# Attention on one Trainium2 core: products with V in one burst, and the transpose of y in y's own bank

## The reference, cut to what matters

```python
q = (xn @ q_w + q_b).reshape(Bx, Tx, H, -1)
k = (xn @ k_w + k_b).reshape(Bx, Tx, H, -1)
att = jnp.einsum('bnhl,bmhl->bnmh', q, k)
att = att + (1.0 - mask) * -1000000.0
att = jax.nn.softmax(att, axis=2)
v = ((xn @ v_w + v_b) * src_mask[:, :, None]).reshape(Bx, Tx, H, -1)
y = jnp.einsum('bnmh,bmhl->bnhl', att, v).reshape(Bx, Tx, Dx)
```

## Time and profile before

| | us |
|---|---|
| median of 3 runs | 7056.02 |
| lowest and highest of them | 7052.95, 7059.61 |
| the profiled execution, its own time | 7056.06 |
| its span in the profile | 7054.2 |

### The profile page before, as it was taken

One profiled execution on the slowest core, in us unless ns is written; L12 is line 12 of the kernel. 1 busy time (PEld: TensorE's weight loads), 2 busy tenths in 40 slices (PEclk: granted clock), 3 DMA queues, 4 the chain that ended last, 5 costly groups with the idle time before them and its releaser, 6 DMA issues.

```text
span 7054.2 us, 136215 instructions
## 1 busy us (share of the span) xinstructions
PE 6300.6 (89%) x43360; PEld 3962.4 (56%) x43360; DVE 5911.7 (84%) x7137; ACT 4676.3 (66%) x6657; POOL 3153.6 (45%) x1541
## 2 busy tenths in 40 slices
PE   6998899988999889989799898998899988999888
PEld 2664457644575546745467455764457544575544
DVE  0787988789897998979888799888988799897985
ACT  2665668567685677847777467765768667685674
POOL 0105871067601775019730388105771067601873
PEclk9999899998999989999899999999899998999989
DMA  3525884368923687237862388525884368923786
GB/s 143 165 81 160 192 209 125 108 162 187 235 76 137 160 200 209 73 134 177 202 181 91 131 197 204 148 87 158 187 209 126 116 159 188 239 68 132 169 195 166
DMA packets 437182, 1108.91 MB, mean 157 GB/s; under 512 B 50185, under 2 KB 50313, under 8 KB 432225
## 3 DMA queue, kind: packets, MB, share of 16 engines
q1 hardware_dynamic: 256672, 671.49, 29.1%
q0 software_dynamic: 161344, 394.81, 28.4%
q10 hardware_dynamic: 18432, 33.56, 1.3%
HBM read 581.17 MB, written 250.10 MB: 118 GB/s over the span
## 4 chain that ended last, share of the span: by engine, by line
PE 62%; issue 14%; DVE 7%; DMA 6%; POOL 5%; ACT 4%; DVEq 0%; SPq 0%; ACTq 0%; POOLq 0%
PE ps L1245 38%; PE ps L1490 10%; PE ps L1354 7%; POOL area_s L699 5%; DMA area_acc<-area_w 4%; PE ps L1295 4%; ACT area_h L839 2%; DMA z_keep<-z_st 2%; DVE area_s L1065 2%; DVE area_h L1182 1%; PE ps L1297 1%; ACT area_s L830 1%; DVE area_dt L1170 1%; PE ps L1439 1%; DVE area_u L1173 1%
## 5 line engine op out<-in xcount | busy, mean ns | idle before, releaser
L699 POOL TENSOR_TENSOR area_s<-area_u,area_s 128x1024 f32<-128x1024 f32 x1024 | 2539.9, 2568 | 553.2 <-DVE area_u L1173 386.6
L1182 DVE TENSOR_TENSOR_SCAN area_h<-ps,area_s 128x1024 f32<-128x1024 f32 x1024 | 2335.2, 2280 | 58.3 <-POOL area_s L699 44.9
L1490 PEld LDWEIGHTS ps<-ident,area_h 128*128 128x128 f32 x8192 | 954.4, 146 | 917.7 <-DVE area_acc L1192 524.9
L830 ACT ACTIVATE area_s<-area_s,negmax 128x1024 f32<-128x1024 f32 x1024 | 1177.7, 1150 | 421.9 <-DVE negmax L1065 421.1
L1490 PE MATMUL ps<-ident,area_h 128*128 128x128 f32 x8192 | 1153.7, 286 | 300.6 <-DVE area_h L1182 205.7
L1065 DVE CUSTOM_DVE_ANT_0 area_s<-ps,area_dt 128x1024 f32<-128x1024 f32 x1024 | 1243.3, 1215 | 113.9 <-PE ps L1245 113.9
L686 POOL TENSOR_TENSOR area_s<-area_s 128x1024 f32<-128x1024 f32 x64 | 176.2, 2753 | 2504.5 <-ACT area_s L874 2504.5
L901 ACT ACTIVATE ps<-area_dt,negA 128x1024 f32<-128x1024 f32 x1024 | 1146.3, 1120 | 221.9 <-DVE area_h L1182 108.0
L887 ACT ACTIVATE area_w<-ps,C_nat 128x512 f32<-128x512 f32 x1024 | 704.4, 688 | 733.2 <-PE ps L1490 685.6
L1354 PE MATMUL ps<-ident,area_s 128*128 128x128 f32 x8192 | 1129.0, 276 | 17.3
L1354 PEld LDWEIGHTS ps<-ident,area_s 128*128 128x128 f32 x8192 | 939.6, 142 | 246.7 <-ACT area_h L839 74.2
(11 more groups left out here) (126 smaller groups left out, 5555.5 us busy)
## 6 DMA issues: line engine op xcount, KB each, us to landing
area_acc<-area_w POOLq DMA_DIRECT2D x256, 1024.0 KB, 8.9
area_s<-b_rows SPq DMA_DIRECT2D x256, 512.0 KB, 5.2
q_stack<-qk_keep SPq DMA_DIRECT2D x520, 128.0 KB, 2.8
k_stack<-qk_keep SPq DMA_DIRECT2D x520, 128.0 KB, 3.1
qk_keep<-q_stack SPq DMA_DIRECT2D x144, 256.0 KB, 4.9
qk_keep<-k_stack SPq DMA_DIRECT2D x144, 256.0 KB, 4.9
area_s<-z_keep SPq DMA_DIRECT2D x72, 512.0 KB, 4.5
y_keep<-area_acc POOLq DMA_DIRECT2D x8, 4096.0 KB, 15.1
```

Source lines behind the costliest of these rows:

```text
L699: pool.tensor_tensor(dbu[:, dl % 2, :], U[:, k // (NS * DL) * DL + dl, :], bb[:, q, :], ALU.mult).then_inc(s_dbu.sem, 1)
L830: nc.scalar.activation(S[:, t % SR, :], S[:, t % SR, :], ACT.Exp, scale=-1.0, bias=negmax[:, t % TILES:t % TILES + 1], accum_out=den[:, t ...
L1182: v.tensor_tensor_scan(out=hs[:, q, dl, :], data0=banks(2 * (dl % 2)), data1=dbu[:, dl % 2, :], initial=0.0, op0=ALU.mult, op1=ALU.add).th ...
L1490: last = nc.tensor.transpose(ps[:, 4 + n % 2, dl * P:(dl + 1) * P], hs[:, r % 2, dl, n * P:(n + 1) * P], ident[:, :])
```

## The change

All eight key tiles of a half's product with V are now issued at step 0 as one burst (64 records), and nothing at steps 1 and 2. The transpose of y no longer takes a bank of the ring: it goes to columns 128 to 255 of bank 6, next to the product with V, and the normalising product reads it there. The ring then has only the two uses for every tile. Since the next half's product writes bank 6 too, its burst waits at step 0 for the normalising product of the half before (`s_yn`).

```diff
--- before.py
+++ after.py
@@ -43,9 +43,7 @@
     order = []
     for t in range(ALL):
         order += [("dve", t), ("act", t)]
-        if t >= 2 * HALF - 1 and t % HALF == HALF - 1:
-            order.append(("y", t // HALF - 1))
-    return order + [("y", ALL // HALF - 1)]
+    return order
 
 
 RING_ORDER = ring_order()
@@ -55,7 +53,7 @@
 def ring_bank(*use):
 
     return RING[RING_AT[use] % len(RING)]
-AV_KEYS = ((0, 1, 2), (3, 4, 5), (6, 7), ())
+AV_KEYS = ((0, 1, 2, 3, 4, 5, 6, 7), (), (), ())
 
 
 N0_STEP, QKV_STEP, QKV_SPAN = 5, 9, 51
@@ -1073,7 +1071,7 @@
                         dve.wait_ge(*s_rd.at(b, half + 1))
                         at = t % TILES
                         v.tensor_tensor(Y[:, hf * HALF:(hf + 1) * HALF, head * HD:(head + 1) * HD],
-                                        ps[:, ring_bank("y", half), 0:P].rearrange("p (c l) -> p c l", l=HD),
+                                        ps[:, 6, P:2 * P].rearrange("p (c l) -> p c l", l=HD),
                                         rden[:, at - 3:at + 1].unsqueeze(2).to_broadcast([P, HALF, HD]), ALU.mult
                                         ).then_inc(s_yn.sem, 1)
                     t = s - C_LAG
@@ -1335,7 +1333,7 @@
                 def ring_free(*use):
                     if RING_AT[use] >= len(RING):
                         who, i = RING_ORDER[RING_AT[use] - len(RING)]
-                        pe.wait_ge(*{"dve": s_pv, "act": s_pa, "y": s_yn}[who].at(b, i + 1))
+                        pe.wait_ge(*{"dve": s_pv, "act": s_pa}[who].at(b, i + 1))
 
                 scores(0)
                 scores(1)
@@ -1362,6 +1360,8 @@
                         if step == 0:
                             pe.wait_ge(*s_pv.at(b, (half + 1) * HALF))
                             pe.wait_ge(*s_pa.at(b, (half + 1) * HALF))
+                            if half:
+                                pe.wait_ge(*s_yn.at(b, half))
                         for m in AV_KEYS[step]:
                             for c in range(HG):
                                 last = mm(ps[c * HD:(c + 1) * HD, 6, 0:P], V[:, m, head * HD:(head + 1) * HD],
@@ -1372,8 +1372,7 @@
                     if t >= 0 and t % HALF == HALF - 1:
                         half = t // HALF
                         pe.wait_ge(*s_yc.at(b, half + 1))
-                        ring_free("y", half)
-                        nc.tensor.transpose(ps[:, ring_bank("y", half), 0:P], yT[:, half % 2, :], ident[:, :]
+                        nc.tensor.transpose(ps[:, 6, P:2 * P], yT[:, half % 2, :], ident[:, :]
                                             ).then_inc(s_yt.sem, 1)
                 pe.wait_ge(*s_yn.at(b, G * HG * 2))
                 norm_pe(n1, b)
```

## The result

The changed kernel takes 7158.21 us (median of 4 runs, 7157.27 to 7160.92) against 7055.46 of the kernel before (7052.95 to 7059.61): a ratio of 1.0147, 95% interval 1.0132 to 1.0162, so 102.75 us or 1.5% slower. The forecast was 7177, slower, with a range of 7070 to 7240.

The account below looks back on a forecast made before the run. PE was taken to bound the attention, DVE close behind. A loop through both engines grew the period from 8.55 to 9.06 us; 29 periods plus 0.3 a batch, times 8, gave 121 us more: 7177, range 7070 to 7240.

Parts of the forecast that it names:

- The saving on PE: Products with V on PE: two of three groups go, 0.30 us each, 0.60 off PE per period.
- Step 1 of the loop: Start of DVE's step 0 reduction, through the normalising product, to the start of PE's burst: 1.49 us.
- Step 2: On PE, from the start of the 64-record burst to the next scores: 1.89 us, bounds 1.79 and 2.16.
- Step 3: From those scores through four transposes to DVE's copy: 1.21 us, with DVE idle for 1.5.
- Step 4: DVE from that copy to the next period: 0.61 to the reduction, then DVE steps of 1.75 and 2.11 us.
- The sum: The whole loop through PE and DVE: a period of 9.06 us against 8.55 before, 0.51 more.
- Head and tail: Each attention batch outside its 29 periods, before and after them: 0.3 us more together.
- The other stages: Kernel stages outside the attention: not edited, no cost, no overlap with the attention's end.
- The added wait: At step 0 PE's burst waits about 0.5 us for DVE's normalising product of the half before.
- the case without any such wait: Rival: the normalising product is done before PE arrives, loop over DVE's copy of y, period 8.60, time 7070; chance 0.08.
- PE stays the bound: Rival: PE's own 7.65 us sets the attention period, 209 us less, 6847; chance 0.07.
- The clock: Rival: the clock falls to 1.2 GHz in stretches, doubling the burst's 1.89 us, over 7400; chance 0.03.

Follow-up runs that it names:

- e4: The change with key tiles back in groups of 3, 3 and 2 and the normalising product ahead of the reduction: 6971.63 us, period 8.21.
- e5: The change with two groups of four key tiles at steps 0 and 2 and the normalising product ahead of the reduction: 6900.78 us, 6899.06 when repeated.
- e8: The kernel before with only the key tiles regrouped, four each at steps 0 and 2, transposed y still in the ring: 6967.90 us, period 8.19.
- e3: The whole change with the normalising product moved ahead of the reduction in the same DVE step: 7047.13 us, period 8.55.
- e2: The change without the burst, groups of 3, 3 and 2 as before, transposed y in bank 6: 7068.42 us, period 8.61.
- e7: The whole change with one extra DVE copy of transposed y right ahead of the normalising product: 7208.87 us, period 9.22.
- e1: The kernel before with only the burst of eight key tiles at step 0, transposed y still in the ring: 7174.38 us, period 9.06.
- e6: The change with two groups of four key tiles at steps 0 and 1 and the normalising product ahead of the reduction: 7031.26 us, period 8.48.

## Why the prediction was right

- **What bounds it.** PE was full, DVE close behind. e4 shows it: with the ring's wait of 0.30 off PE's path, and no other wait put in its place, the same groups of 3, 3 and 2 take 8.21 instead of 8.55.
- **The saving on PE.** A group has a fixed cost and the records have a rate: put at 0.30 and 0.0275 us. e5 has one group less than e4 and is 0.33 us a period faster; e8 against before 0.36. The saving is real, and the change has it too: PE's busy time fell. The changed kernel spends it, and more, on waiting.
- **Step 1 of the loop**, reduction to burst, put at 1.49: 1.58. The latency of 0.06 from DVE's end to PE's load was right within 0.05 (the load starts at 1204.81, 0.11 behind the end at 1204.70), and the matmuls start 0.04 after the load. PE's wait was put at about 0.5: from start to start it is 2.01 - 1.53 = 0.48 (e3), in the profile's idle time 0.41 on the matmuls and 0.62 on the loads.
- **Step 2**, burst to scores, put at 1.89: 1.88. The bounds of 1.79 and 2.16 were further apart than they had to be. The trace of before has a whole half in one piece, at the end of the batch, where no scores come between; the prediction did not use it:

```profile
1329.39 1.96 PE L1245 MATMUL ps<-area_h,area_u 128*32 128x128 f32 x64 [0.67 <-ACT area_h L839]
```

  Its 1.96 us is the busy time of 64 records, as in the changed kernel; less the 0.07 by which a group's busy time passes the start of the next scores (0.86 against 0.79, rows 5) it gives 1.89 without any extrapolation.
- **Step 3**, scores to DVE's copy, put at 1.21 with DVE idle for 1.5: 1.21 and 1.50.
- **Step 4** holds the largest miss: 0.61 and 1.75 were right (0.61, 1.74), but DVE's last step was put at 2.11 and takes 2.00. The stretch of before from which 2.11 comes contains a short wait that the view doesn't print. Here are its two rows:

```profile
1209.80 0.17 DVE L1088 RECIPROCAL rden<-den 128x4 f32<-128x4 f32 x1
1209.96 0.69 DVE L1095 COPY area_h<-ps 128x512 f32<-128x512 f32 x1
```

  The copy follows the reciprocal by 0.16, and in the changed kernel by 0.08 (1211.63 to 1211.71). It starts 1.20 behind the scores of its step (1208.76, rows 5), about the same 1.21 as the copy at 1205.53, which is printed as waiting for PE. In e2, e4 and e5 it also starts 1.20 or 1.21 behind the scores. So 2.11 was a duration with a wait in it: 0.08 of the 0.11, and the other 0.03 is the copy itself, busy 0.66 instead of 0.69.
- **The sum.** 9.02 instead of 9.06, and that it came so near is in part luck: step 1 was 0.09 too short and step 4 0.12 too long. The rest lies outside the periods. Head and tail were put at 0.3 us a batch together; from the first scores of a batch to its last transpose of y, the eight batches take 106.0 us more, of which the 29 periods of each make 107.4, so head and tail together give 0.2 us a batch back. The other stages were put at nothing and take 3.2 us less (102.8 in all between the two profiled executions); the stretch between two attentions varies from 563.3 to 567.1 us in the kernel before, so that is within its scatter. The forecast of 121 us was 18 too much: about 11 from the period, 4 from head and tail, 3 from the other stages. Measured are 103, with an interval of 93 to 114.
- **The added wait.** It was named as the thing that closes the loop, and e3 and e7 show that. That the burst costs without it too, by coming to the same time with another wait, is shown by e1; the prediction had put the case without any such wait at 8.60, and e3 measures 8.55. Every kernel with y in bank 6 keeps the wait for the normalising product; whether the kernel could do without it, no run shows.
- **The rivals.** That PE stays the bound would have needed 7.65. With the burst no kernel came near: the fastest, e3, takes 8.55, and e5, with two groups, 7.88. The clock didn't fall: it is 1.00 in the attention before and after.
- **What was wrong among the signs**: PE's busy share was put near 84% and is 235.45 / 261.53 = 90% in the attention. 7.65 us was what PE needs from start to start, but a busy time also counts the tails of the matmuls, which overlap the next start unless a wait stands there. In a light step of the changed kernel PE is busy for 1.60 us (1209.82 to 1211.42) before its wait, where such a step takes 1.37 from start to start. DVE's share, 83%, was right.
- **The rule on changes of mode** (the Trainium skill, "TensorEngine Tiling (Array Packing)", Key Properties) says that a change of the tiling mode drains TensorE, and gives no price. The traces agree as far as a fixed cost goes: each group has a change on either side and costs about 0.3 us beyond its records, and the loads stand idle for 0.17 us ahead of it (e3, 1125.99) and for 0.20 behind it (1206.73 in the changed kernel). If this saving alone had counted, 0.6 us, the change would have been faster; the trace shows 0.47 a period slower, because the work that was put together had kept PE and DVE in step (e5 against e6).

What stays open: how much of a group's fixed cost is the drain on its two sides and how much is something else; no run takes them apart. That the depth of two score buffers is what couples the engines is read from the waits and the starts; a burst with the scores or the ring buffered more deeply was not tried, since the kernel has no bank left for it (0 to 3 hold scores, 4, 5 and 7 are the ring, 6 holds y).

## What to carry to other kernels

Where two engines hand tiles to each other through two buffers, look at the balance within those two steps and not only within a period: bunching work that one of them had spread out can cost more than it saves, even if both have slack on average. Here the same two groups take 7.88 us a period with a step between them and 8.48 side by side. To forecast it, walk one period as a loop from start to start through both engines; a wait inside the loop costs in full although both engines idle elsewhere. And when a wait appears because a buffer is now shared, look for the instruction that frees it and ask whether it can go ahead of its neighbours: here that was worth 1.3 to 1.6%.

## What was unexpected

One line of a table (e8) brings 1.3% to the kernel before, and with y in bank 6 and the product ahead (e5) 2.2%: two groups of four key tiles, set apart by an empty step. The balanced form of the changed kernel also shows that the added wait has nearly the same price wherever the work stands: 0.47 us a period with the burst (9.02 to 8.55), 0.40 with 3, 3, 2 (8.61 to 8.21), 0.41 with 4, 0, 4, 0 (8.29 to 7.88). And a copy of 128x128 that is 0.29 us busy delays what stands behind it on DVE by only 0.20 (1121.96 to 1122.16 in e7).
